# Rows for the experts' tiles gathered from token rows, with the copy of W1 on ScalarE

## What is computed

```python
logits = _gelu(x @ rw1) @ rw2
probs = jax.nn.softmax(logits, axis=-1)
wgt, idx = jax.lax.top_k(probs, TOP_K)
out = jnp.zeros_like(x)
for e in range(E):
    Ye = _gelu(x @ w1[e] + b1[e]) @ w2[e] + b2[e]
    Ce = _gelu(b1[e]) @ w2[e] + b2[e]
    for k in range(TOP_K):
        mask = idx[..., k] == e
        active = jnp.any(mask).astype(x.dtype)
        term = jnp.where(mask[..., None], Ye, Ce)
        out = out + active * wgt[..., k:k + 1] * term
```

## Time and profile before

| | us |
|---|---|
| median of 3 runs | 502.76 |
| lowest, highest | 502.70, 503.56 |
| the profiled execution | 503.75 |
| its span, first to last instruction | 502.0 |

### The profile page before, as it was taken

One profiled execution on the slowest core, in us unless ns is written; L12 is line 12 of the kernel. 1 busy time (PEld: TensorE's weight loads), 2 busy tenths in 40 slices (PEclk: granted clock), 3 DMA queues, 4 the chain that ended last, 5 costly groups with the idle time before them and its releaser, 6 DMA issues.

```text
span 502.0 us, 7227 instructions
## 1 busy us (share of the span) xinstructions
PE 399.3 (80%) x2560; PEld 347.3 (69%) x2560; DVE 373.4 (74%) x532; ACT 251.6 (50%) x493; POOL 88.0 (18%) x84
## 2 busy tenths in 40 slices
PE   3998573898813038999999999999977897999664
PEld 3997441777612028999999999999956775787422
DVE  5999876994576978778877787589343477789885
ACT  6988753788831044433443344244223355485553
POOL 2000102000036820000000000197566000000000
PEclk9999887998955559999999999999976997999957
DMA  8900000000573110841161682560023000000000
GB/s 294 367 33 1 2 0 0 1 1 0 172 270 138 63 63 22 271 139 42 33 210 33 207 300 104 139 208 21 22 74 107 0 0 1 10 12 10 12 10 31
DMA packets 29505, 42.99 MB, mean 86 GB/s; under 512 B 2440, under 2 KB 24600, under 8 KB 29344
## 3 DMA queue, kind: packets, MB, share of 16 engines
q1 hardware_dynamic: 18528, 26.54, 15.5%
q10 hardware_dynamic: 9376, 11.80, 7.3%
q0 software_dynamic: 1568, 4.20, 2.7%
HBM read 33.10 MB, written 9.44 MB: 85 GB/s over the span
## 4 chain that ended last, share of the span: by engine, by line
PE 56%; DVE 21%; issue 11%; ACT 7%; POOL 2%; DMA 2%; ACTq 0%; POOLq 0%; SPq 0%; DVEq 0%
PE bank L1487 18%; PE bank L1468 17%; PE bank L1533 7%; PE bank L1341 3%; PE bank L1542 2%; PE bank L1312 2%; DVE scr L765 2%; DVE scr L767 2%; PE bank L1460 1%; PE bank L1359 1%; DVE scr L817 1%; DMA v<-in_kT 1%; POOL small L345 1%; DVE small L1221 1%; DVE w3T L783 1%
## 5 line engine op out<-in xcount | busy, mean ns | idle before, releaser
L1468 PE MATMUL bank<-big,yT 128*128 x384 | 86.7, 379 | 0.0
L581 ACT ACTIVATE yT<-bank,big 128x128 f32<-128x128 f32 x192 | 54.5, 369 | 54.6 <-PE bank L1487 48.7
L1468 PEld LDWEIGHTS bank<-big,yT 128*128 128x128 f32 x384 | 71.2, 190 | 8.7
L1533 PE MATMUL bank<-yT,scr 128*128 128x256 f32 x192 | 47.7, 408 | 3.5 <-DVE yT L1160 2.8
L1533 PEld LDWEIGHTS bank<-yT,scr 128*128 128x128 f32 x192 | 39.0, 207 | 10.0 <-issue 3.2
L345 POOL TENSOR_TENSOR small<-small 128x2 f32<-128x2 f32 (+1 forms) x9 | 10.1, 1121 | 190.2 <-DVE small L1187 83.7
L590 ACT ACTIVATE yo<-bank 128x256 f32<-128x256 f32 x24 | 9.2, 383 | 53.6 <-PE bank L1468 53.6
L1312 PE MATMUL bank<-identf,scr 128*128 128x128 f32 x240 | 30.7, 287 | 3.8 <-DVE scr L778 3.8
L1487 PEld LDWEIGHTS bank<-ygT,w3T 128*128 128x128 f32 x256 | 31.8, 203 | 2.3 <-issue 2.0
L1487 PE MATMUL bank<-ygT,w3T 128*128 128x128 f32 x256 | 32.0, 287 | 1.6 <-ACT ygT L573 1.6
L1312 PEld LDWEIGHTS bank<-identf,scr 128*128 128x128 f32 x240 | 29.9, 204 | 4.1 <-DVE scr L778 4.0
(11 more groups left out here) (327 smaller groups left out, 861.4 us busy)
## 6 DMA issues: line engine op xcount, KB each, us to landing
big<-in_moe_w SPq DMA_DIRECT2D x16, 1024.0 KB, 6.3
slot_rows<-zeros SPq DMA_DIRECT2D x1, 3072.0 KB, 13.3
xg<-slot_rows ACTq DMA_DIRECT2D x24, 128.0 KB, 2.1
slot_outputs<-yo ACTq DMA_DIRECT2D x24, 128.0 KB, 2.4
v<-in_kT SPq DMA_DIRECT2D x2, 512.0 KB, 4.6
big<-in_gateT SPq DMA_DIRECT2D x1, 1024.0 KB, 7.1
big<-in_upT SPq DMA_DIRECT2D x1, 1024.0 KB, 9.2
big<-in_downT SPq DMA_DIRECT2D x1, 1024.0 KB, 11.7
```

The source lines that it names most:

```text
L581: ins = sc.activation(hT[j % 2][:, c], ps[1 + 2 * (j % 2) + c // 4][:, (c % 4) * P:(c % 4 + 1) * P], ACT.Gelu, bias=b1s[:, c, j:j + 1])
L1468: ins = te.matmul(ps[5 + 2 * (j % 2)][:, 0:C], hT[j % 2][:, c], big[:, bass.ds(at + (W2_AT + c * C), C)], start=(c == 0), stop=(c == IC - 1))
L1533: ins = te.matmul(bank_of((p, c))[:, m * 256:(m + 1) * 256], qgu[:, m, k, c * P:(c + 1) * P], yT[:, k, 256 * p:256 * (p + 1)], start=(k == ...
```

## The change

1. `y1` is stored by SP in HBM as token rows, row 0 being zeros (4 DMAs of two tiles each, on SP's queue ahead of the first bias and the experts' weights). The zero fill of 3 MB is gone. There is no scatter. For each tile POOL gathers 128 rows by an index list `rowi` straight into `xg`, three tiles ahead at most; slots that no token takes read row 0.
2. The index lists are the slots inverted: DVE makes 0/1 matrices from the slots (`in_tile`, `holds`, `in_slot`), PE multiplies them (16 small matmuls into bank 6), and DVE turns the result into integers after `table`.
3. `copy_w1` goes from DVE to ACT: the first two ahead of the Gelu table load, then one for each tile, between `copy_xT` and `store_yo`. The loads of `xg` on ACT's queue are gone.
4. DVE computes the ratios 4 to 7 in one go (`late_ratio`), without steps and all with its own reciprocal; POOL's part of ratio 4 and ACT's Ln and Exp are gone. DVE alone quantizes the weights of layer 3.
5. The gates are turned inside the tiles 1 and 2 (`turn_gates`, `copy_gcT`), not ahead of the loop. The turned bias goes to bank 5. Two loads of later weights are issued one tile earlier.

```diff
-        XG = nc.dram_tensor("slot_rows", (TILES * P, C), F32, kind="Internal").ap()
+        Y1 = nc.dram_tensor("token_rows", (1 + NT, C), F32, kind="Internal").ap()
...
-            sp.dma_start(XG.rearrange("(n p) c -> p n c", p=P),
-                         zeros[:].unsqueeze(1).to_broadcast([P, TILES, C])).then_inc(s["zero_fill"], 16)
-
+            sp.dma_start(Y1[0:1, :], zeros[0:1, :]).then_inc(s["zero_row"], 16)
+
+            for b in range(T // 2):
+                sp.wait_ge(s["y1_ready"], b + 1)
+                sp.dma_start(Y1[1 + 2 * b * P:1 + (2 * b + 2) * P, :].rearrange("(t p) c -> p t c", p=P),
+                             y1[:, 2 * b:2 * b + 2]).then_inc(s["y1_stored"], 16)
             sp.wait_ge(s["x_l0"], T)
...
+            link(gp.iota(rowi[:, 0:1].bitcast(I32), pattern=[[0, 1]], base=1, channel_multiplier=1))
+            gp.tensor_copy(iota_p[:, 1:2], rowi[:, 0:1].bitcast(I32))
+            link(gp.iota(xg[:, 0, 0:P].bitcast(I32), pattern=[[1, P]], base=0, channel_multiplier=0))
+            gp.tensor_copy(iota_r[:], xg[:, 0, 0:P].bitcast(I32))
+            link(gp.iota(xg[:, 1, 0:2 * T].bitcast(I32), pattern=[[0, 2], [1, T]], base=0, channel_multiplier=0))
+            gp.tensor_copy(iota_i[:], xg[:, 1, 0:2 * T].bitcast(I32).rearrange("p (k t) -> p k t", k=2))
...
-            def make_g(n):
-                l, k = (n // KC) % 2, n % KC
-                pool.wait_ge(s["euk_ready"], n + 1)
-                link(gp.tensor_tensor(g[:, l, k], g[:, l, k], ek[:, k], ALU.subtract))
-                gp.tensor_tensor(gv, g[:, l, k], v[:, k], ALU.mult).then_inc(s["gv_ready"], 1)
...
-            make_g(4)
-
-            pool.wait_ge(s["pos_ready"], 1)
-            pool.wait_ge(s["y1_ready"], T // 2)
-            pool.wait_ge(s["zero_fill"], 16)
-            for i in range(T):
-                for k in range(2):
-                    gp.indirect_dma_start(out=XG, out_offset=bass.IndirectOffsetOnAxis(ap=posi[:, k, i:i + 1], axis=0),
-                                          in_=y1[:, i], in_offset=None).then_inc(s["scattered"], 16)
+            pool.wait_ge(s["y1_stored"], 16 * (T // 2))
+            pool.wait_ge(s["zero_row"], 16)
+            pool.wait_ge(s["rows_ready"], 1)
+            for j in range(TILES):
+                if j >= 3:
+                    pool.wait_ge(s["xt_ready"], j - 2)
+                gp.indirect_dma_start(out=xg[:, j % 3], out_offset=None, in_=Y1,
+                                      in_offset=bass.IndirectOffsetOnAxis(ap=rowi[:, j:j + 1], axis=0)).then_inc(ld_xg[j % 3], 16)
+            for j in range(3):
+                pool.wait_ge(ld_xg[j], 16 * (TILES // 3))
...
-            for h in range(2):
+            def copy_gcT(h):
                 act.wait_ge(s["gcT_tr"], h + 1)
-                sc.activation(gcT[:, h * 512:(h + 1) * 512], ps[4 + h][0:2 * E, :], ACT.Copy).then_inc(s["gcT_ready"], 1)
-            act.wait_ge(s["den_ready"], 1)
-            link(sc.activation(ratio[:, 1, 0], den[0], ACT.Ln))
-            sc.activation(ratio[:, 1, 0], ratio[:, 1, 0], ACT.Exp, scale=-1.0).then_inc(s["inv_ready"], 1)
-
+                sc.activation(gcT[:, h * 512:(h + 1) * 512], ps[6][0:2 * E, :], ACT.Copy).then_inc(s["gcT_ready"], 1)
+
+            def copy_w1(j):
+                at = act.value_load(table[0:1, j:j + 1], min_val=0, max_val=(RING - 1) * EW)
+                landed = act.value_load(table[0:1, TILES + j:TILES + j + 1], min_val=32, max_val=32 * E)
+                act.wait_ge(s["ld_w"], landed)
+                if j >= 3:
+                    act.wait_ge(s["ps1_ready"], 2 * (j - 3) + 2)
+                elif j == 2:
+                    act.wait_ge(s["y1_stored"], 16 * (T // 2))
+                sc.activation(w1c[j % 3], big[:, bass.ds(at, W2_AT)], ACT.Copy).then_inc(s["w1_ready"], 1)
+
+            act.wait_ge(s["table_ready"], 1)
+            copy_w1(0)
             act.wait_ge(s["b1_turned"], 1)
-            sc.activation(b1s, ps[6][:, 0:IC * TILES].rearrange("p (c j) -> p c j", c=IC), ACT.Copy).then_inc(s["b1s_ready"], 1)
+            sc.activation(b1s, ps[5][:, 0:IC * TILES].rearrange("p (c j) -> p c j", c=IC), ACT.Copy).then_inc(s["b1s_ready"], 1)
+            copy_w1(1)
             sc.preload_act_table(ACT.Gelu)
-            act.wait_ge(s["scattered"], 16 * 2 * T)
-
-            def load_xg(j):
-                if j >= 3:
-                    act.wait_ge(s["xt_ready"], j - 2)
-                act.dma_start(xg[:, j % 3], XG[j * P:(j + 1) * P, :]).then_inc(ld_xg[j % 3], 16)
...
-            for j in range(3):
-                load_xg(j)
...
             for j in range(TILES):
                 if j == 15:
                     load_w3()
+                elif j == 17:
+                    load_rows()
                 elif j == 18:
-                    load_rows()
-                elif j == 19:
                     load_l2()
                 gelu_tile(j)
                 if j + 1 < TILES:
                     copy_xT(j + 1)
-                if j + 3 < TILES:
-                    load_xg(j + 3)
+                if j + 2 < TILES:
+                    copy_w1(j + 2)
                 if j >= 1:
                     store_yo(j - 1)
+                if j in (1, 2):
+                    copy_gcT(j - 1)
...
+            def late_ratio(n):
                 l, k = n // KC, n % KC
-                if of_den:
-                    link(ve.tensor_scalar(decay[:], template[:], ew[:, l, k:k + 1], None, ALU.mult))
-                src, fwd, bwd = (ek, den[n % 2], db) if of_den else (ekv, ratio[:, l % 2, k], nb)
-                ve.tensor_tensor_scan(fwd, decay[:, 0:NT], src[:, k], 0.0, ALU.mult, ALU.add)
-                ins = ve.tensor_tensor_scan(bwd[:, ::-1], decay[:, NT:0:-1], src[:, k, ::-1], 0.0, ALU.mult, ALU.add)
-                link(ins)
-
-            def sums(n):
-
-                l, k = n // KC, n % KC
-                num = ratio[:, l % 2, k]
-                ve.tensor_tensor(den[n % 2], den[n % 2], db[:], ALU.add)
+                num, gk = ratio[:, l % 2, k], g[:, l % 2, k]
+                link(ve.tensor_scalar(decay[:], template[:], ew[:, l, k:k + 1], None, ALU.mult))
+                ve.tensor_tensor_scan(df, decay[:, 0:NT], ek[:, k], 0.0, ALU.mult, ALU.add)
+                ve.tensor_tensor_scan(db[:, ::-1], decay[:, NT:0:-1], ek[:, k, ::-1], 0.0, ALU.mult, ALU.add)
+                ve.tensor_tensor_scan(num, decay[:, 0:NT], ekv[:, k], 0.0, ALU.mult, ALU.add)
...
+                dve.wait_ge(s["euk_ready"], n + 1)
+                link(ve.tensor_tensor(gk, gk, ek[:, k], ALU.subtract))
+                ins = ve.tensor_tensor(gv, gk, v[:, k], ALU.mult)
+                if n == 2 * L - 1:
+                    ins.then_inc(s["ek_free"], 1)
+                link(ve.tensor_tensor(df, df, db[:], ALU.add))
                 link(ve.tensor_tensor(num, num, nb[:], ALU.add))
-                dve.wait_ge(s["gv_ready"], n - 3)
-                link(ve.tensor_tensor(den[n % 2], den[n % 2], g[:, l % 2, k], ALU.add))
-                ve.tensor_scalar(den[n % 2], den[n % 2], 1e-8, None, ALU.max).then_inc(s["den_ready"], 1)
-                ve.tensor_tensor(num, num, gv, ALU.add).then_inc(s["gv_used"], 1)
-
-            def finish_ratio(n, factor):
-                l, k = n // KC, n % KC
-                num = ratio[:, l % 2, k]
-                if n == 4:
-                    dve.wait_ge(s["gv_used"], 1)
+                link(ve.tensor_tensor(df, df, gk, ALU.add))
+                if n == 2 * L - 1:
+                    dve.wait_ge(s["ek_free"], 1)
+                link(ve.tensor_tensor(num, num, gv, ALU.add))
+                link(ve.tensor_scalar(df, df, 1e-8, None, ALU.max))
+                link(ve.reciprocal(df, df))
                 for b in range(B):
                     c = slice(b * S, (b + 1) * S)
...
+                    ins = ve.scalar_tensor_tensor(num[:, c], df[:, c], tf[:, 3, b:b + 1], num[:, c], ALU.mult, ALU.mult)
                 ins.then_inc(s["ratio_ready"], 1)
                 dve.wait_ge(s["ratio_ready"], n - 3)
...
+            flat = posf.rearrange("p k t -> p (k t)")
+            link(ve.tensor_scalar(slot_of[:, 0], flat, 1.0 / P, -0.5 + 1.0 / 256, ALU.mult, ALU.add))
+            link(ve.tensor_scalar(slot_of[:, 0], slot_of[:, 0], MAGIC, MAGIC, ALU.add, ALU.subtract))
+            ve.scalar_tensor_tensor(slot_of[:, 1], slot_of[:, 0], -float(P), flat, ALU.mult, ALU.add)
+            link(ve.tensor_tensor(in_tile, iota_t[:].unsqueeze(1).to_broadcast([P, 2 * T, TILES]),
+                                  slot_of[:, 0].unsqueeze(2).to_broadcast([P, 2 * T, TILES]), ALU.is_equal))
+            ve.tensor_tensor(holds[:, :, 0], in_tile, iota_i[:].rearrange("p k t -> p (k t)").unsqueeze(2).to_broadcast([P, 2 * T, TILES]), ALU.mult)
+            ve.tensor_scalar(holds[:, :, 1], in_tile, iota_p[:, 1:2], None, ALU.mult).then_inc(s["b_ready"], 1)
+            for k in range(2):
+                c = slice(k * T, (k + 1) * T)
```

(61 more changed lines are left out.)

104 lines of the change are left out of this document (35 added, 69 removed).

## The result

The changed kernel takes 481.13 us (median of four runs, 480.05 to 481.68) against 502.73 for the kernel before on the same chip: ratio 0.9565, 95% interval 0.9545 to 0.9586. The forecast was 482.7. The profiled execution took 480.05 with a span of 478.3. First some lines of the page: the granted clock in 40 slices and the group of gathers (columns: count, busy us and mean ns of one, idle us ahead of them and its releaser).

The account below looks back on a forecast made before the run. PE was taken to bound the tile loop at 7.25 us a tile, and a chain of routing, scatters and ACT's load to hold up tile 0. 502.76 - 20.95 + 0.9 = 482.7 us; range 478.5 to 490.

Parts of the forecast that it names:

- Part 2: Between slots and table: new index-list operations on DVE add 4.5 us (2.8 to 6); table's own chain stays 2.45.
- Part 4: Ahead of tile 0: ACT's queue is late next; up(0) at 164.15 against 185.12, a gain of 20.95 us.
- Part 1: In the routing: without POOL's work on ratio 4, two small DVE operations shorten, gaining 4.35 us on the chain.
- Part 3: Ahead of tile 0: one gather replaces 16 scatters on the chain; first rows land near 159 us.
- The rule weighed there: GpSimd shares SBUF interfaces with VectorE, so two-input DVE instructions slow gathers; first rows 1.7 us later, sum unchanged.
- Part 5: In the loop: gate transposes on PE's path lose 0.9 us; ACT's work stays beside PE.
- The unoverlapped sum of 6.9: In the loop: ACT's work per tile with nothing overlapped, 6.9 us, under PE's period of 7.25.
- Part 6: Covers: SP's later weight loads, DVE's ratios and quantizing, and POOL's bias work cost nothing.
- (a): Rival: chain ahead of tile 0 is longer, through late gather, ACT's loads or DVE's operations; 484.5 to 490; chance 0.24.
- (d): Rival: first tile still starts near 180 because something else in the routing releases it; 498 to 502; chance 0.03.
- (b): Rival: less time; PE's clock rises sooner, up to 2 us, cheap compares 1.7 more; 479 to 481; chance 0.13.
- (c): Rival: ACT becomes the loop's bound if its serial work exceeds 7.25 us a tile; 507 if loads drain ACT; chance 0.05.

Follow-up runs that it names:

- pool_ratio4: The changed kernel with POOL again computing the two operations of ratio 4 beside the routing, as before: 484.23 us, ratio 0.9631.
- lnexp4: The changed kernel, gather kept, with ACT again doing Ln and Exp of ratio 4 ahead of its Gelu table: 498.48 us, ratio 0.9930.
- gates_early: The changed kernel with both groups of gate transposes moved ahead of the first x_transpose: 478.07 us, ratio 0.9497.
- copy_twice: The changed kernel with ACT making each copy of W1 twice from tile 2 on: 482.64 us, ratio 0.9617.
- copy_thrice: The changed kernel with ACT making each copy of W1 three times from tile 2 on: 520.17 us, ratio 1.0372.
- after_again: The changed kernel run once more, unedited, in more rounds: 480.01 us, ratio 0.9547 to the kernel before.

## Why the prediction was right

**The result** lay 1.6 us under the forecast. By the columns 0.64 of that is Part 2 and 0.79 Part 4. The total and its parts came out, but one reading behind them was wrong: which chain held tile 0 back. On the prediction's own steps:

- **Part 1** (4.35 expected): 4.35. The earlier trace rows had the two long operations and their short second pass; `pool_ratio4` shows the cause.
- **Part 2** (4.5): 3.86. The operations of 384 columns took 0.55, 0.56 and 0.31, those of 1024 columns 1.17 each. From slots to the end of the last of them it was 4.06, a term of 4.5 over-sized by 0.44, and the table's own chain took 2.25 in place of 2.45, the difference lying in one operation of 24 columns, 0.41 beside the first scatter (153.25 in before) and 0.18 now. The table came at 153.27 against 154.75; the rest of that is the 0.83 of the earlier router.
- **Part 3** (rows land near 159): the gather started at 154.68, took 1.19 on POOL, and PE turned the rows from 158.30 to 158.99. All 24 gathers, as the view of that line gives them for the kernel after:

```profile
L364 POOL DMA_INDIRECT xg<-token_rows,rowi x24: 944/1099/2658, 154.7 to 304.4; - x24
...
DMA to landing us min/median/max: 2.7/4.0/7.3
```

944 to 2658 ns against 956 to 2619 for the scatters: same price, other count on the chain. Even the slowest landing is half of the 14 us that three buffers give, and PE waited for the first gather alone. The long gathers have a pattern in the timeline of after. The three beside an idle DVE and the five that began beside a DVE operation with one input, reciprocal or reduction, took 0.94 each. Of the thirteen beside two-input operations of 1024 columns or more, eleven took 1.03 to 2.66 and two 0.94 and 0.95. One of 2.24 stands beside a long one-input TENSOR_SCALAR, and the first two (1.19, 0.97) beside small operations. The rule weighed there (the Trainium skill, GPSIMD Engine Reference, 8. Key points) agrees with most of these rows and had no influence on the time. The prediction's "two-input ratios beside every gather" was too much: a ratio holds a reciprocal of 6.55 us, and the ratios ended at 260.9.
- **A step that the prediction had wrong.** It held the scatters to be what kept tile 0 back, and traced the chain through them. The chain of waits of before goes another way, over ACT's Ln, the table load and Exp for ratio 4 and the Gelu table load, which ended at 184.58; the scattered rows had been turned 1.07 earlier. By `lnexp4` the gather without item 4 of the change is worth 0.10 us, where the prediction's Part 3 and 4 would have given it everything. The sum came out because item 4 removed the second chain too, because 185.12 was a time read from the trace and not derived from the scatters, and because the prediction priced the new queue on ACT as it stands in the changed program. It was right about what remains. That the change as a whole took away both chains, of which it had seen one, was luck.
- **Part 4** (9.4 from table to `up(0)`): 8.61. Register loads ahead of the first copy 1.43 (153.27 to 154.70) against 1.47. From the end of PE's turn of the bias (156.92) to the second copy (158.13) it was 1.21, with the bias copy in it, against 0.35 + 1.47; this is most of the 0.79. Copies 1.91 against 2.0; table load 1.28 as before. (158.95 + 1.47 + 2.0 is 162.42 and not the 162.35 written there, which moves the forecast by 0.07.) By the figure of the Trainium skill (DMA: Bandwidth & Descriptors, Latency and other measured facts), some 600 ns for a load, two would take 1.2, an estimate. The second pair agrees with it only if the loads ran under the copy of the bias, for the engine itself stood for 0.84 between the two, and no row shows when they started.
- **Part 5** (+0.9): +0.87, and `gates_early` takes exactly that back. Register loads in the loop cost ACT nothing: the copy starts 0.02 behind `copy_xT` (203.55 + 0.40, 203.97), so the queue does run ahead of the engine as the earlier trace rows let one expect. The unoverlapped sum of 6.9 was about 4.9 in fact. Missing in it were the ten loads of later weights on ACT's queue, five of them in one tile, where ACT stands for 2.9 us; under cover here, not in `copy_twice`.
- **Part 6** (nothing): SP's stores went out at 127.79 and the first weights at 131.82. DVE's ratios and quantizing, POOL's bias work: none of them released PE in the window from 182.5 to 325.
- **Rivals.** (a) and (d) had no part in it. Of (b), the operations of the index lists were 0.4 cheaper together and not 1.7, the two long compares 0.05 of it; `up(0)` to `up(1)` took 6.95 in place of 7.49, which is within the 6.7 to 8.3 of the other executions and shows no gain from the clock. (c) is excluded as the kernel stands, and its decision point bracketed by `copy_twice` and `copy_thrice`.

## What to carry to other kernels

When one wait goes, list every chain that ends at the same instruction: the view of waits names only the last, and here two of almost equal length stood ahead of tile 0. Either edit alone brought 0.1 or 1.75 us from slots to first tile, both together 18.1, so someone who had tried the gather alone would have dropped it. When a gain is split into stages, check that an instruction moved across a boundary does not change the split: here the index lists moved `table` and made the third column 3.9 us too good. Work moved onto another engine's queue was free here while that engine's serial work of a cycle stayed under the bound's, except where its DMA issues came on top; doubling the moved instruction showed the distance at once. Where a change gives a fixed latency back, look at what is next in the newly binding queue: moving one copy behind two other instructions gave another 2.3 us.

## What the runs showed of the hardware

- A DVE operation of 64 columns with two inputs takes 0.23 us alone and 2.38 to 2.43 us beside a POOL operation of 1024 columns with two inputs, that is as long as POOL's own (2.34 to 2.36), in before and in `pool_ratio4` alike.
- The DVE comparison of 1024 columns with 2-byte output and, by the program, one 2-byte and one 4-byte input (L1029) takes 1.17 us, an all 4-byte operation of that size 1.22; the smaller type brought almost nothing here.
- With unchanged code, PE's granted clock differs from execution to execution. In after and `after_again`, the same kernel, `up(0)` to `up(1)` took 6.95 and 7.39 us, the stretch behind the last `down` 138.49 and 136.57 (mean granted clock 0.86 and 0.88), and the router started at 136.94 and 138.44; the four columns repeated within 0.03. Four matmuls of one group show it, first in after, then in `after_again`:

```profile
64.06 1.02 PE L1298 MATMUL bank<-big 128*128 128x512 bf16 x4 [0.88 <-DVE big L890]
```

```profile
63.96 1.87 PE L1298 MATMUL bank<-big 128*128 128x512 bf16 x4 [0.88 <-DVE big L890]
```

The first ran at the full clock (1.00 from 63 to 66 us), the second at half (0.50). The idle time directly ahead is the same 0.88, but ahead of the group before it PE had stood for 1.06 us in after and for 3.29 in `after_again`.
